# The step sizes' cap on ScalarE, the expert routing behind the first and around the fourth scan, and the bias products in the second state

## The reference

```python
x = x + mixer(layernorm(x))        # selective scan, 512 channels, 16 states
x = x + cross_attention(layernorm(x), ctx)
x = x + experts(layernorm(x))      # 8 experts, the best 2 of each token

# the mixer
xz = x @ W_in; xp, z = split(xz)
xc = silu(causal_conv(xp, conv_w, conv_b))
Bm, Cm = split(xc @ W_x)
dt = softplus(xc @ W_dt + b_dt)
h = exp(dt * A) * h + (dt * xc) * Bm      # a scan over the 1024 tokens
y = (h * Cm).sum() + D * xc
out = (y * silu(z)) @ W_out

# the experts
nf = rms_norm(x) * norm_weight            # bf16
scores, idx = top_k(nf @ gate.T + gate_bias, 2); w = softmax(scores)
out = sum over experts of combine(idx, w) * (act(nf @ mlp1 + bias1) @ mlp2 + bias2)
```

## Time and profile before

| what | value |
| --- | --- |
| median of 3 runs | 1564.02 us (1562.88 to 1570.86) |
| the profiled execution's own time | 1570.56 us |
| its span, first to last instruction | 1568.8 us |
| mean granted TensorE clock | 0.909 |
| busy: VectorE, TensorE, GpSimd, ScalarE | 1369.4, 1228.8, 966.1, 938.5 us |

### The profile page before, as it was taken

How to read it: one execution, slowest core, us unless ns; L and a number is a source line. 1 busy time by engine, 2 the same in 40 slices (tenths; PEclk the granted TensorE clock), 3 DMA queues, 4 the chain that set the end, 5 groups by cost and what they waited for, 6 DMA issues and landing times. The chain is left out here.

```text
span 1568.8 us, 22313 instructions
## 1 busy us (share of the span) xinstructions
PE 1228.8 (78%) x5883; PEld 846.4 (54%) x5942; DVE 1369.4 (87%) x1815; ACT 938.5 (60%) x1394; POOL 966.1 (62%) x529
## 2 busy tenths in 40 slices
PE   5856667789677887899787788799777787786797
PEld 2344445655455555676365555576355555576465
DVE  5589999788899999898899999988889999974687
ACT  3354454344677777725577777725577877732554
POOL 1388888413698989622689888731688989821000
PEclk9889998999699989999789989999889989998799
DMA  7011121401121121221112122221111212230121
GB/s 224 29 47 34 54 68 34 159 11 56 41 74 67 54 79 63 80 78 56 41 48 74 47 59 98 92 78 52 45 48 47 72 49 69 79 104 28 48 61 53
DMA packets 76603, 102.06 MB, mean 65 GB/s; under 512 B 9180, under 2 KB 54117, under 8 KB 76526
## 3 DMA queue, kind: packets, MB, share of 16 engines
q1 hardware_dynamic: 71372, 97.36, 19.7%
q10 hardware_dynamic: 5154, 3.78, 0.7%
HBM read 82.69 MB, written 18.43 MB: 64 GB/s over the span
## 5 line engine op out<-in xcount | busy, mean ns | idle before, releaser
L1384 DVE TENSOR_TENSOR_SCAN work<-ps,work 128x1024 f32<-128x1024 f32 x192 | 438.7, 2285 | 37.7 <-ACT ps L970 27.0
L1836 PE MATMUL ps<-ident,work 128*128 128x128 f32 x1536 | 304.2, 321 | 185.5 <-DVE stage L1428 72.3
L1836 PEld LDWEIGHTS ps<-ident,work 128*128 128x128 f32 x1536 | 192.9, 160 | 319.1 <-DVE stage L1428 121.5
L970 ACT ACTIVATE ps<-dt,a_neg 128x1024 f32<-128x1024 f32 x256 | 285.8, 1118 | 131.0 <-DVE work L1384 84.2
L716 POOL TENSOR_TENSOR work<-dtu,b_bc 128x1024 f32<-128x1024 f32 x124 | 289.8, 2366 | 48.6 <-PE ps L1836 47.6
L1428 DVE SCALAR_TENSOR_TENSOR stage<-ps,c_tok,stage 128x512 f32<-128x512 f32 x384 | 272.1, 734 | 18.8 <-PE ps L1836 16.7
L1858 PE MATMUL ps<-w,work 128*128 (+1 forms) x1024 | 255.0, 395 | 2.0 <-DVE work L1568 2.0
L1858 PEld LDWEIGHTS ps<-w,work 128*128 128x128 f32 x1024 | 198.7, 198 | 40.2 <-issue 3.6
L732 POOL TENSOR_TENSOR stage<-stage,work 128x512 f32<-128x512 f32 x128 | 160.3, 1276 | 41.6 <-ACT work L986 41.6
L1808 PE MATMUL ps<-nfT,w 128*128 128x512 bf16 x453 | 151.6, 422 | 38.8 <-DVE work L1498 24.2
L716 POOL TENSOR_TENSOR work<-dtu,w_out 128x1024 f32<-128x1024 f32 x64 | 149.3, 2355 | 45.8 <-PE ps L1836 45.8
(11 more groups left out here) (172 smaller groups left out, 1952.3 us busy)
## 6 DMA issues: line engine op xcount, KB each, us to landing
b_bc<-b_rows SPq DMA_DIRECT2D x32, 512.0 KB, 4.1
w_out<-b_rows SPq DMA_DIRECT2D x32, 512.0 KB, 4.6
wbc<-combine_rows SPq DMA_DIRECT2D x64, 256.0 KB, 3.8
work<-z_rows SPq DMA_DIRECT2D x8, 1024.0 KB, 6.3
z_rows<-mix SPq DMA_DIRECT2D x24, 256.0 KB, 2.7
stage<-in_x SPq DMA_DIRECT2D x8, 512.0 KB, 4.9
xt<-in_x SPq DMA_DIRECT2D x8, 512.0 KB, 4.7
x_rows<-xt SPq DMA_DIRECT2D x4, 1024.0 KB, 4.2
```

Of the source, the lines that this page charges most:

```text
L970: act.activation(decay_in(d, alone, opening), dt[:, d, :], ACT.Exp, scale=a_neg[:, bass.ds(it * 2 + (d * N + hf * (N // 2) + par), 1)]).th ...
L1384: dve.tensor_tensor_scan(h, decays, h, 0.0, ALU.mult, ALU.add).then_inc(scan_done, 1)
L1836: mm = pe.transpose(ps[:, a % HT_BANKS, d * P:(d + 1) * P], slot(par, d)[:, a * P:(a + 1) * P], ident[:, :])
```

## The change

The cap goes from VectorE to ScalarE: a Relu out of PSUM with scale -1 and bias 30 - b_dt, and the Exp then has scale -1 and bias 30. Each step size is Relu, Exp and Ln in one line (`softplus`). On TensorE S0 to S3 come first, then N0, S4, S5, N1, S6, G and S7; the two N jobs of a half of the tokens become one job with one copy. S7 is in bank 6. On VectorE the scores stand behind scan 0, the ranks between the last scans' input and scan 3, the weights behind scan 3. CT stays at TensorE's end of the tail, with the experts' first up products now ahead of it; ScalarE copies it in the loop's first body (`keep_rows`). The bias product of the first half goes from the loop's start to state 1 (the second state), in front of its down products. One load of b is issued ahead of the combine rows, GpSimd's last norm scale comes behind the first dt * xc, and the small tiles of the routing lie elsewhere in `work`. Context lines are cut from the diff.

```diff
--- before.py
+++ after.py
@@ -84,7 +84,8 @@
         iota = sb("iota", [P, 1, E])
-        shift = sb("shift", [P, 3])
+        shift = sb("shift", [P, 4 + CT])
+        cap_bias = shift[:, 4:4 + CT]
@@ -144,7 +145,7 @@
         nf = work[:, 5120:6144].bitcast(BF16).rearrange("p (a d) -> p a d", a=TT)
-        o = [6144]
+        o = [8192]
@@ -315,14 +317,16 @@
                 return [(kind, c * TH + a, 0) for a in range(TH)]
+            if kind == "N":
+                return [(kind, 0, c)]
             return [(kind, k, c) for k in range(CT if kind == "Y" else DK)]
         head = both("Y") + both("O")
-        tail = ([("B", 0, 0), ("C", 0, 0)] + steps[0:2] + tiles_of("N", 0) + steps[2:3] + tiles_of("N", 1) +
-                steps[3:4] + [("G", 0, 0)] + steps[4:] + [("CT", 0, c) for c in halves])
+        tail = ([("B", 0, 0), ("C", 0, 0)] + steps[0:4] + tiles_of("N", 0) + steps[4:6] + tiles_of("N", 1) +
+                steps[6:7] + [("G", 0, 0)] + steps[7:] + [("CT", 0, c) for c in halves])
         all_jobs = (head + both("T") + x_jobs((0, 1)) + both("T2") + x_jobs((2, 3)) + both("Q") + both("PT") +
@@ -340,8 +344,7 @@
-        late_banks = {**dict(zip(steps, (2, 3, 4, 5, 6, 7, 0, 1))),
-                      **{("N", k, c): (6, 0)[c] + k for c in halves for k in range(DK)}, ("G", 0, 0): 0,
+        late_banks = {**dict(zip(steps, (2, 3, 4, 5, 6, 7, 0, 6))), ("N", 0, 0): 0, ("N", 0, 1): 1, ("G", 0, 0): 1,
                       ("CT", 0, 0): 6, ("CT", 0, 1): 7}
@@ -349,7 +352,7 @@
         dve_order = (both("Y") + both("O") +
-                     both("Q") + both("V") + [("C", 0, 0)] + steps[0:3] + [("G", 0, 0)] + steps[3:])
+                     both("Q") + both("V") + [("C", 0, 0)] + steps[0:4] + [("G", 0, 0)] + steps[4:])
@@ -551,6 +554,8 @@
                         load_b(b, 0, 0, par)
+                    if r is not None:
+                        load_b(b, 0, 1, 0)
                 if r is not None:
@@ -592,11 +597,12 @@
-                def loads(hf, first, last, opening=False, turning=False):
+                def loads(hf, first, last, opening=False, turning=False, begun=False):
                     with sp.Fori(first, last) as it:
                             if b is not None and not opening:
-                                load_b(b, hf, it, par)
+                                if not (begun and par == 0):
+                                    load_b(b, hf, it, par)
                                 if hf == 0 and par == 0:
@@ -611,7 +617,8 @@
                 loads(0, 0, 1, True)
-                loads(0, 1, ITS)
+                loads(0, 1, 2, begun=b is not None and bp is not None)
+                loads(0, 2, ITS)
@@ -650,7 +657,7 @@
             pool.sem_inc(evict_added, EVICTED)
-            for i, value in enumerate((-LIMIT, ALPHA / 2 * LIMIT, 2 * LIMIT)):
+            for i, value in enumerate((-LIMIT, ALPHA / 2 * LIMIT, 2 * LIMIT, STEP_CAP)):
                 pool.memset(shift[:, i:i + 1], value).then_inc(shift_set, 1)
@@ -686,9 +693,10 @@
                 if r is not None:
-                    for n in (2, 3):
-                        for c in halves:
-                            norm_scale(n, r, c)
+                    for n, c in ((2, 0), (2, 1), (3, 0)):
+                        norm_scale(n, r, c)
+                    if b is None:
+                        norm_scale(3, r, 1)
                 if b is not None:
@@ -698,6 +706,8 @@
                                                ALU.mult).then_inc(dtu_ready[0], 1)
+                            if r is not None and i == 0:
+                                norm_scale(3, r, 1)
                             if c == NH - 1:
@@ -834,16 +844,27 @@
-                def soft_exps(*batch):
-                    for i in batch:
-                        act.wait_ge(cap_ready, b * CT * NH + i + 1)
-                        act.activation(soft[:, i, :], soft[:, i, :], ACT.Exp).then_inc(soft_exp, 1)
-                def soft_logs(*batch):
-                    for i in batch:
-                        act.wait_ge(soft_exp, b * CT * NH + i + 1)
-                        act.activation(soft[:, i, :], soft[:, i, :], ACT.Ln, bias=1.0).then_inc(soft_ready, 1)
+                def softplus(i):
+                    d = steps[i][1]
+                    if i == 0:
+                        act.wait_ge(shift_set, 4)
+                        act.wait_ge(cap_set, 1)
+                    ph.wait_mm(act, steps[i])
+                    act.activation(soft[:, i, :], ph.bank(steps[i]), ACT.Relu, scale=-1.0, bias=cap_bias[:, d:d + 1]
+                                   ).then_inc(cap_ready, 1)
+                    act.wait_ge(cap_ready, b * CT * NH + i + 1)
+                    act.activation(soft[:, i, :], soft[:, i, :], ACT.Exp, scale=-1.0, bias=shift[:, 3:4]
+                                   ).then_inc(soft_exp, 1)
+                    act.wait_ge(soft_exp, b * CT * NH + i + 1)
+                    act.activation(soft[:, i, :], soft[:, i, :], ACT.Ln, bias=1.0).then_inc(soft_ready, 1)
+                def sum_squares(c):
+                    for a in range(c * TH, (c + 1) * TH):
+                        act.wait_ge(x16_ready, r * TT + a + 1)
+                        act.activation(square[:, a, :], xc16[:, a, :], ACT.Square, accum_out=ssq[:, a:a + 1]
+                                       ).then_inc(ssq_ready, 1)
@@ -851,11 +872,11 @@
                 def experts_in(c):
-                    for _, k, _ in tiles_of("N", c):
-                        ph.wait_mm(act, ("N", k, c))
-                        act.activation(nfT[:, k, c * HALF:(c + 1) * HALF],
-                                       ph.bank(("N", k, c)).bitcast(BF16)[:, 0:HALF], ACT.Copy
-                                       ).then_inc(act_freed, 1)
+                    job = ("N", 0, c)
+                    ph.wait_mm(act, job)
+                    act.activation(nfT[:, :, c * HALF:(c + 1) * HALF],
+                                   ph.bank(job).bitcast(BF16).rearrange("p (k t) -> p k t", k=DK), ACT.Copy
+                                   ).then_inc(act_freed, 1)
@@ -910,47 +931,35 @@
                 if r is not None:
-                    for a in range(TT):
-                        act.wait_ge(x16_ready, r * TT + a + 1)
-                        act.activation(square[:, a, :], xc16[:, a, :], ACT.Square, accum_out=ssq[:, a:a + 1]
-                                       ).then_inc(ssq_ready, 1)
-                if b is not None:
-                    for i in (0, 1):
-                        soft_exps(i)
-                        soft_logs(i)
+                    sum_squares(0)
+                if b is not None:
+                    softplus(0)
+                    softplus(1)
+                if r is not None:
+                    sum_squares(1)
+                if b is not None:
+                    softplus(2)
+                    opening_decay(0)
+                    softplus(3)
                 if r is not None:
                     experts_in(0)
-                if b is not None:
-                    opening_decay(0)
-                    soft_exps(2)
-                    soft_logs(2)
-                if r is not None:
                     experts_in(1)
                 if b is not None:
-                    soft_exps(3)
-                    soft_logs(3)
+                    softplus(4)
+                    opening_decay(1)
                 if r is not None:
                 if b is not None:
-                    opening_decay(1)
-                    for i in (4, 5):
-                        soft_exps(i)
-                        soft_logs(i)
+                    softplus(5)
                     opening_decay(2)
-                    for i in (6, 7):
-                        soft_exps(i)
-                        soft_logs(i)
-                if r is not None:
-                    for c in halves:
-                        ph.wait_mm(act, ("CT", 0, c))
-                        act.activation(rows[32:32 + E, c * HALF:(c + 1) * HALF], ph.bank(("CT", 0, c))[0:E, :],
-                                       ACT.Copy).then_inc(act_freed, 1)
-                if b is not None:
+                    softplus(6)
+                    softplus(7)
                     opening_decay(3)
                     act.preload_act_table(ACT.Exp)
+                else:
+                    keep_rows(ph)
                 if b is None:
@@ -962,6 +971,13 @@
                         wait_apart(act, b_stored, (b + 1) * (QUARTERS * 16))
+            def keep_rows(ph):
+                for c in halves:
+                    ph.wait_mm(act, ("CT", 0, c))
+                    act.activation(rows[32:32 + E, c * HALF:(c + 1) * HALF], ph.bank(("CT", 0, c))[0:E, :],
+                                   ACT.Copy).then_inc(act_freed, 1)
@@ -1063,6 +1079,7 @@
                             clip(s * 2 + 1)
+                            keep_rows(phase_between(b))
                         else:
@@ -1210,12 +1227,6 @@
-                def cap(i):
```

(64 more changed lines are left out.)

19 lines of the change are left out of this document (10 added, 9 removed).

## The result

The changed kernel takes 1599.99 us (median of 4 executions, 1599.02 to 1600.38), the kernel before 1563.54 beside it (median of 4). The ratio is 1.0205, 95% interval 1.0184 to 1.0227: 2% slower. The forecast was 1591, range 1569 to 1602. The profiled execution took 1599.02 us, span 1597.2, mean granted clock 0.906.

The account below looks back on a forecast made before the run. TensorE's start on state 0, more than VectorE's load, was taken to set the loop's clock. 3 x (7.6 + 2.1) - 2.7 + 0.4 = 26.8 us on the median of 1564.02 gave 1590.8 us; own range 1583 to 1601, with rivals 1569 to 1602.

Parts of the forecast that it names:

- TensorE's chain sets the loop's clock: From state 0's transposes to state 1's second scan: TensorE's start on state 0 sets the loop, more than VectorE's load.
- Short VectorE instructions are held by GpSimd: Routing around scan 3: cast, compares and small products wait for GpSimd's running instruction; combine weights ready only at 417.3.
- Rival A: Routing in the double tails: short instructions aren't held, second eviction only 1.6 us late; 1573 us, chance 15%.
- Cap on ScalarE: 1.4 us left of 5.3 in each tail, 2.7 in the first: Step sizes in the tails: VectorE's 5.3 us relief mostly goes into waiting, 1.4 left; first tail gains 2.7.
- N1 and G hold ScalarE and VectorE: Second tail: ScalarE waits 5 us for N1's copy; VectorE, behind scan 0, waits for G until 391.8.
- Chain 7.6 us late: TensorE behind the routing: transposes of state 0 wait for CT, so its own tiles and the chain come 7.6 us late.
- the first boundary: End of a GpSimd instruction at 406.2: the cast gets in there or at 408.5; scan 3 taken at 411.2, between 408.9 and 413.4.
- Bias product 2.1 us: Eight matmuls ahead of state 1's down products are exposed: 3.77 us from above, 1.9 at the upper clock, 2.1 taken.
- Joined N, early load of b, norm scale, small tiles: nothing: Tail parts covered by TensorE's 3.5 us per product, so no effect; uncovered, the norm scale would cost 1.1 us.
- The sum: Whole kernel: three double tails at 7.6 + 2.1, less 2.7 in the first tail, plus 0.4 in the last, 26.8 us.

Follow-up runs that it names:

- e3: Changed kernel with GpSimd's four products of state 1 held back until the combine weights are ready; 1573.1 us, 1.0056 of the kernel before.
- e5: Changed kernel with TensorE's job N1 ahead of S5 and the gate product G ahead of S6; 1590.2 us, 1.0155 of the kernel before.
- e7: Kernel before with only the cap moved from VectorE to ScalarE; 1557.2 us, 0.9943 of the kernel before.
- e1: Changed kernel with the first half's bias products left out, so part of the output is wrong; 1580.5 us, 1.0100 of the kernel before.
- e2: Changed kernel with the first half's bias products moved ahead of the transposes of tiles 6 and 7 in state 1; 1583.8 us, 1.0124 of the kernel before.
- e9: Changed kernel with GpSimd's wait, N1 and G one step-size product earlier, and the bias product in state 1's gap; 1557.3 us, 0.9946 of the kernel before.

## Why the prediction was right, point by point

The direction and its main reason, held routing in front of TensorE's chain, were right. The closeness of the number owes something to luck: 36 us were measured for 27, the bias was sized too low and the chain too high, and the two errors nearly cancel. The forecast's own range, by its parts (3 x 3.6 us below, 3 x 3.2 above), should have been 1580 to 1600, not 1583 to 1601; 1599.99 lies at its very end.

- **TensorE's chain sets the loop's clock**: shown. TensorE waits 17.05 us for the weights, and e3 to e5, which bring them forward, bring the loop forward.
- **Short VectorE instructions are held by GpSimd**: shown by e3. Rival A, that they are not, fell: the compares had never met GpSimd before, and took 4.44 us. The Trainium skill (SBUF — State Buffer, Who interferes with whom) has it that a VectorE instruction with two SBUF inputs is fully blocked by a GpSimd instruction that reads SBUF and issued first; the trace agrees, 4.44 us for 0.36.
- **Cap on ScalarE: 1.4 us left of 5.3 in each tail, 2.7 in the first**: the first tail gained 2.5 (from the transposes of C to scan 3, 34.27 us for 36.76). In the second, the last scan's input starts 1.8 earlier, counted from ScalarE's copy of B. The Relu out of PSUM took 0.68 us where the nearest row had 0.69. The Trainium skill (ScalarE: Activation LUTs, Rules for kernel authors) puts relu, min and add on VectorE and gives a figure for bf16. This cap is fp32, 0.74 us on VectorE, and e7 is faster without it there, so here the rule is not borne out.
- **N1 and G hold ScalarE and VectorE**: right, 4.80 and 4.55 us of idle, 2.9 in the end (e5).
- **Chain 7.6 us late**: somewhat too much. Behind scan 0, state 0's second eviction came 5.0 us later and state 1's second scan 4.2; scan 0 itself came 1.1 later in tail 3, and 2.1 in the second tail counted from ScalarE's copy of B. Together 5.3 to 6.3. The cast got in at the first boundary, where the forecast took a middle between its cases.
- **Bias product 2.1 us**: the term that was mis-sized. State 1's second scan to state 2's first is 5.6 longer (17.8 for 12.2), and e1 takes 5.2 of it out again. The forecast counted on the clock rising no later than before, 7.4 us behind state 1's second scan (421.1 to 428.5); it rose 14.7 us behind it (423.8 to 438.5), in the middle of z. So the bound from above, the 3.78 of the product alone, was too low as well: down products and z lost 0.88 and 0.91 on top.
- **Joined N, early load of b, norm scale, small tiles: nothing**: not tried one by one. The forecast had scan 0 some 0.8 us later; it came 2.1 later behind ScalarE's copy of B. The forecast kept its holds to the routing, and the rows show one more, in the second half of the expert input (4.75 us for 2.68). The cause is read from rows and not tried.
- **The sum.** Against the second trace of the kernel before, the span is 35.9 us longer for 26.8 forecast. Cut at row starts it is 2.3 up to row 1's first scan (forecast -1.9), 11.1, 10.2 and 9.4 for the three rows with double tails (9.7, 9.7 and 8.9), and 2.9 behind (0.4). The two misses in the rows, some +10 for the bias and some -8 for the chain, nearly cancel, which is luck. Of the 6.7 outside them a part is scatter, since the two traces of the kernel before differ by 3.7 and 3.1 in these very parts; how much is not settled.

## What to carry to other kernels

Ask of each VectorE instruction on SBUF operands what GpSimd is doing when it asks: one of 0.14 us took 2.12 here, and two in a row took 4.44 for 0.36. The searches and scans ran beside GpSimd unharmed. Either put the others where GpSimd is idle, or make GpSimd wait: 4.85 us of idle time in each of three tails bought 27 us, 17 of them by the hold itself. And price a matmul that is put in front of a serial chain at the lower clock, with what it does to the clock of the products behind it; in a gap of the same state most of its cost was covered (e2 is 3.2 us above the kernel without it, for 19.5). A change of many parts can be slower as a whole with a part in it that is faster: run the parts alone.

## What was not expected of the hardware

TensorE was busy for 10.9 of 12 us from 426 to 438 in the changed kernel and its granted clock was 0.50 all the while; the eight bias matmuls, with 8 rows of weights, were in it. In the kernel before it rose at 428.5, after 4.5 us of which TensorE was busy for nearly all. In e9, with the same matmuls 6 us ahead of the down products, it was back by the time of these, which took 1.95 us. The bias matmuls don't hold the clock down by themselves: in e3's third and fourth tails they ran with it back, in 2.15 and 2.20 us, behind the same instructions that left it at 0.50 in the second, where they took 3.78. So the price of a product in this place changes by over 1.5 us between tails of one execution, and what decides it was not found.
